# Norm statistics, scan outputs and expert answers moved off VectorE in a four-stage audio tower

## The reference

```
h  = frames(x) @ DCT.T                                  # tokens
u  = layernorm(h)
a  = u + [mamba2(u) , flip(mamba2(flip(u)))] @ proj.T   # two scans, 4 heads, 16 states
h2 = h + layernorm(a)*g + b
y  = sum over the top 2 of 8 experts: w_e * (gelu(layernorm(h2) @ w1_e) @ w2_e)
h3 = h2 + y
h3 = h3 + window_attention(layernorm(h3))               # 8 keys, softmax
h4 = h3 + top-k network(layernorm(h3))                  # keeps 64 of 512, 128 of 256, 64 of 512
```

## Time and profile before

| | us |
|---|---|
| three runs | 8032.64, 7994.39, 8031.15 (median 8031.15) |
| profiled execution, its own time | 8044.3 |
| its span | 8042.4 |
| busy: PE, DVE, ACT, POOL | 6126.0 (76%), 6747.5 (84%), 3593.5 (45%), 2468.3 (31%) |
| mean granted TensorE clock | 0.867 |

### The profile page before, as it was taken

The page is one execution under the profiler, slowest core; times in us unless marked ns, Lnnn a source line. Parts: engine busy times, 40 slices in busy tenths (PEclk is TensorE's granted clock), DMA queues, the critical chain, the costliest instruction groups (busy, mean ns, idle before and its releaser), DMA issues.

```text
span 8042.4 us, 115198 instructions
## 1 busy us (share of the span) xinstructions
PE 6126.0 (76%) x34088; PEld 4811.3 (60%) x34088; DVE 6747.5 (84%) x21836; ACT 3593.5 (45%) x7726; POOL 2468.3 (31%) x2872
## 2 busy tenths in 40 slices
PE   6777787877787777777777778777778777778643
PEld 5656666656666656666656666666666666666422
DVE  2368889888888888889888889888988888888897
ACT  2344445444445444445444445444445444445321
POOL 2233332233332233332233332323332333332220
PEclk8888898888888888898888899888889888889766
DMA  2322222222222222222222222221222222222200
GB/s 71 112 72 67 67 86 78 66 68 67 67 86 78 66 69 65 66 86 79 65 72 65 66 84 79 72 71 59 66 82 79 75 69 63 64 81 80 68 6 4
DMA packets 342571, 560.36 MB, mean 70 GB/s; under 512 B 33728, under 2 KB 261792, under 8 KB 341664
## 3 DMA queue, kind: packets, MB, share of 16 engines
q10 hardware_dynamic: 152576, 357.68, 14.1%
q1 hardware_dynamic: 168992, 153.83, 7.0%
q0 software_dynamic: 20480, 41.98, 1.8%
HBM read 484.63 MB, written 68.74 MB: 69 GB/s over the span
## 4 chain that ended last, share of the span: by engine, by line
PE 36%; DVE 27%; ACT 15%; issue 10%; POOL 6%; ACTq 4%; DMA 2%; POOLq 0%; DVEq 0%; SPq 0%
DVE m L1230 6%; PE pM L656 6%; PE pS L547 5%; PE pM L667 4%; PE pA L709 4%; DVE work L1233 3%; POOL rows L449 3%; DVE sorted L1260 2%; DVE work L1263 2%; ACT hid L915 2%; DVE a L1233 2%; ACTq L895 2%; PE pS L609 2%; PE pS L601 2%; PE pA L721 2%
## 5 line engine op out<-in xcount | busy, mean ns | idle before, releaser
L1230 DVE MAX8 m<-work 128x8 f32<-128x512 f32 x1792 | 1143.6, 680 | 1.0
L547 PE MATMUL pS<-u_fm,wconv_s 128*128 128x315 f32 x3072 | 1015.0, 485 | 94.1 <-ACT xs L860 87.0
L1233 DVE MATCH_REPLACE8 work<-m,work 128x512 f32<-128x512 f32 x1536 | 1026.6, 676 | 0.0
L656 PE MATMUL pM<-turned,expert 128*128 128x128 f32 x4352 | 675.3, 304 | 409.5 <-ACT turned L928 399.2
L410 POOL TENSOR_TENSOR yg<-xs,zs 128x525 f32<-128x525 f32 (+1 forms) x256 | 195.9, 797 | 2489.8 <-ACT xs L870 2489.8
L656 PEld LDWEIGHTS pM<-turned,expert 128*128 128x128 f32 x4352 | 606.2, 213 | 522.5 <-issue 492.5
L547 PEld LDWEIGHTS pS<-u_fm,wconv_s 128*128 128x128 f32 x3072 | 654.0, 217 | 404.6 <-issue 128.3
L915 ACT ACTIVATE hid<-pM,expert 128x128 f32<-128x128 f32 x2176 | 623.2, 372 | 250.5 <-PE pM L656 249.0
L1230 DVE MAX8 m<-a 128x8 f32<-128x512 f32 x768 | 505.4, 679 | 187.9 <-issue 180.9
L667 PE MATMUL pM<-expert,hid 128*128 128x128 f32 x4352 | 629.1, 292 | 0.0
L1263 DVE MATCH_REPLACE8 work<-sorted,work 128x128 f32<-128x128 f32 x2240 | 591.6, 276 | 0.0
(11 more groups left out here) (255 smaller groups left out, 14526.7 us busy)
## 6 DMA issues: line engine op xcount, KB each, us to landing
expert<-in_experts ACTq DMA_DIRECT2D x544, 578.0 KB, 4.0
ab<-decay_rows SPq DMA_DIRECT2D x384, 230.7 KB
rows<-routed_rows SPq DMA_DIRECT2D x128, 256.0 KB, 3.6
answer_rows<-turned ACTq DMA_DIRECT2D x256, 128.0 KB, 3.9
x_sb<-in_x SPq DMA_DIRECT2D x32, 256.0 KB
out<-hk SPq DMA_DIRECT2D x32, 256.0 KB
routed_rows<-un,slot POOLq DMA_INDIRECT x320, 2.2
rows<-answer_rows,slot POOLq DMA_INDIRECT x320, 2.6
```

Of the source, the lines that this page charges most:

```text
L547: last = nc.tensor.matmul(pS[:, 512 * (n % 3):512 * (n % 3) + HQ], wt, tap(d, i, half * HQ, HQ), start=(j == 0), stop=(j == len(blocks) - 1))
L656: last = nc.tensor.matmul(pM[:, bank(i) + j * P:bank(i) + (j + 1) * P], w1_of(i, j), turned[:, (i + 2) % 4, 1, :], start=True, stop=True)
L1230: link(nc.vector.max(m8[:, i, :], now[i]), len(tiles) - 1)
L1233: link(nc.vector.match_replace(work[i], m8[:, i, :], now[i], GONE), len(tiles) - 1)
```

## The change

A helper `act_moments` on ScalarE replaces `moments` on VectorE at four of its five calls (h, h2, h3 twice); the call on `ub` stays. The scan outputs are scaled by ten ScalarE copies into `zs` and added by two GpSimd additions. The gathered answers are weighed by ten ScalarE copies in place and added by two GpSimd additions. All five order strings are new. `x_in` and other semaphores keep their use; `sum1` to `sum3`, `dir_out`, `scaled` and `h3_part` are new.

```diff
+        def act_moments(act, i, first, b, src, spare, var):
+            done = G[f"sum{i + 1}"]
+            for t in range(TILES):
+                last = nc.scalar.activation(spare[:, t, :], src[:, t, :], ACT.Copy, accum_out=lnsum[i][:, 0, t:t + 1])
+            last.then_inc(done.s, 1)
+            act.wait_ge(done.s, done(b, first + 1))
+            nc.scalar.activation(nmean[i][:], lnsum[i][:, 0, :], ACT.Copy, scale=-1.0 / P).then_inc(done.s, 1)
+            act.wait_ge(done.s, done(b, first + 2))
+            for t in range(TILES):
+                last = nc.scalar.activation(spare[:, t, :], src[:, t, :], ACT.Square, bias=nmean[i][:, t:t + 1], accum_out=lnsum[i][:, 1, t:t + 1])
+            last.then_inc(done.s, 1)
+            act.wait_ge(done.s, done(b, first + 3))
+            nc.scalar.activation(vare[i][:, 0:TILES], lnsum[i][:, 1, :], ACT.Identity, bias=c("eps"), scale=1.0 / P).then_inc(var.s, 1)
 def act_stage1
+            act.wait_ge(G["h_sb"].s, G["h_sb"](b, 1))
+            act_moments(act, 0, 0, b, h, u, G["var1"])
...
+            act.wait_ge(G["o_ps"].s, G["o_ps"](b, 1))
+            act.wait_ge(G["rstd1"].s, G["rstd1"](b, 2))
+            for k in range(2 * TILES):
+                d, t = divmod(k, TILES)
+                last = nc.scalar.activation(zs4[:, d, 0, tok(t)], pS[:, tok(k)], ACT.Copy, scale=rstd[0][:, k:k + 1])
+            last.then_inc(G["dir_out"].s, 1)
 def act_stage2
+            act.wait_ge(G["h1_done"].s, G["h1_done"](b, 1))
+            act_moments(act, 1, 0, b, h2, un, G["var2"])
...
+            act.wait_ge(gathered.s, gathered(b, 160))
+            for k in range(2 * TILES):
+                last = nc.scalar.activation(rows[:, k, :], rows[:, k, :], ACT.Copy, scale=top8[:, k % TILES, k // TILES:k // TILES + 1])
+            last.then_inc(G["scaled"].s, 1)
 def act_stage3
+            act.wait_ge(G["u4T_ps"].s, G["u4T_ps"](b, 0))
+            act.wait_ge(G["moe_done"].s, G["moe_done"](b, 1))
+            act_moments(act, 2, 0, b, h3, u3, G["var3"])
...
+            act.wait_ge(G["h3_done"].s, G["h3_done"](b, 2))
+            act_moments(act, 2, 3, b, h3, u3, G["var3"])
 def pool_stage1
+            pool.wait_ge(G["dir_out"].s, G["dir_out"](b, 1))
+            for d in range(2):
+                pool.wait_ge(G["ub"].s, G["ub"](b, d + 1))
+                nc.gpsimd.tensor_tensor(ub[:], ub[:], zs4[:, d, 0, :].rearrange("p (t d) -> p t d", t=TILES), ALU.add).then_inc(G["ub"].s, 1)
 def pool_stage2
+            pool.wait_ge(G["scaled"].s, G["scaled"](b, 1))
+            pool.wait_ge(G["h3_kept"].s, G["h3_kept"](b, 0))
+            pool.wait_ge(G["u4_done"].s, G["u4_done"](b, 0))
+            nc.gpsimd.tensor_tensor(h3[:], h2[:], rows[:, 0:TILES, :], ALU.add).then_inc(G["h3_part"].s, 1)
+            pool.wait_ge(G["h3_part"].s, G["h3_part"](b, 1))
+            nc.gpsimd.tensor_tensor(h3[:], h3[:], rows[:, TILES:, :], ALU.add).then_inc(G["moe_done"].s, 1)
 def dve_stage1
-            dve.wait_ge(G["h_sb"].s, G["h_sb"](b, 1))
-            moments(link, 0, h, G["var1"])
...
-            dve.wait_ge(G["ub"].s, G["ub"](b, 1))
-            dve.wait_ge(G["rstd1"].s, G["rstd1"](b, 2))
-            for d in range(2):
-                for t in range(TILES):
-                    k = d * TILES + t
-                    last = nc.vector.scalar_tensor_tensor(ub[:, t, :], pS[:, tok(k)], rstd[0][:, k:k + 1], ub[:, t, :], ALU.mult, ALU.add)
-                link(last)
+            dve.wait_ge(G["ub"].s, G["ub"](b, 3))
             moments(link, 0, ub, G["var1"])
 def dve_stage2, dve_stage3: three more calls of moments go, and
-            for t in range(TILES):
-                last = nc.vector.scalar_tensor_tensor(h3[:, t, :], rows[:, t, :], top8[:, t, 0:1], h2[:, t, :], ALU.mult, ALU.add)
-            link(last)
-            for t in range(TILES):
-                last = nc.vector.scalar_tensor_tensor(h3[:, t, :], rows[:, TILES + t, :], top8[:, t, 1:2], h3[:, t, :], ALU.mult, ALU.add)
-            last.then_inc(G["moe_done"].s, 1)
```

```diff
-ACT_ORDER = ("44144121211411111411131114113144141111131141131124111322411211121111214112421312142141142112211223111122"
-             "31124244444444244242222422324222432444243224244334444433")
-DVE_ORDER = ("342414424142141142444444444414414444141114111441111111411114111414444444341444414444444344344344342")
-POOL_ORDER = ("21312111313323131")
+ACT_ORDER = ("44443124131333342131311231114111111411411111114111111124111111111111111314413341111424211414122211212131"
+             "23234444144242424234224224224222242222422322244222244444444424")
+DVE_ORDER = ("4444444444141112424342444114141111144414141411411141114311111343444444444144444444444444444414")
+POOL_ORDER = ("3213233111311213211")
...
```

More of the change, by code:

```diff
@@ L61 @@
     ("convb", 6), ("dskip", 4), ("normw", 4), ("projb", P), ("lng", P), ("lnb", P),
-    ("gate_w", E), ("gate_b", E), ("tail", AW * TAIL), ("pos", AW), ("bk", 1),
+    ("gate_w", E), ("gate_b", E), ("tail", AW * TAIL), ("pos", AW), ("bk", 1), ("eps", 1),
     ("wq", P), ("wk", P), ("wv", P),
@@ L77 @@
 COUNTS = dict(
-    x_in=32, xT_ps=1, xT_sb=1, h_ps=1, h_sb=1, var1=3, rstd1=3, u_done=1, uT_ps=1, u_sb=1,
+    sum1=3, sum2=3, sum3=6, x_in=32, xT_ps=1, xT_sb=1, h_ps=1, h_sb=1, var1=3, rstd1=3, u_done=1, uT_ps=1, u_sb=1,
     dt_ps=1, dt_arg=3, dt_act=3, dA_ps=1, dA_sb=1, dA_out=16, ab0=48, ab1=48, ab2=48, ab3=48, proj_ps=HALF_UNITS, proj_sb=HALF_UNITS,
     scanned=12, mix_ps=12, m_done=12, y_ps=12, y_tmp=12, y_gated=2, pad_zero=1, y_sq=2,
-    o_ps=1, ub=1, r_norm=1, attn_scaled=2, h1_done=1,
+    o_ps=1, ub=3, dir_out=1, r_norm=1, attn_scaled=2, h1_done=1,
     var2=1, rstd2=1, u2_done=1, u2T_ps=2, u2T_sb=2, gate_ps=1, gate_arg=1, gate_exp=1,
     chosen=1, rank_ps=1, tiles_done=1, slots_done=1, rows0=48, rows1=32, turned_ps=2, turned_sb=2,
-    expert0=96, expert1=96, expert2=80, hid_ps=MT, hid_sb=MT, tile_done=MT, kept=MT, y_out0=80, y_out1=64, moe_done=1,
+    expert0=96, expert1=96, expert2=80, hid_ps=MT, hid_sb=MT, tile_done=MT, kept=MT, y_out0=80, y_out1=64, scaled=1, h3_part=1, moe_done=1,
     var3=2, rstd3=2, u3_done=1, u3T_ps=2, u3T_sb=2, qkv_ps=6, qkv_sb=6, lg_max=1, lg_done=1, lg_exp=1, den_ps=2, den_sb=2, den_done=1, weighted=2, val_ps=2, att_done=2,
@@ L183, in audio_tower @@
         h = sb("h", [P, TILES, P])
+        lnsum = [sb(f"lnsum{i}", [P, 2, TILES]) for i in range(3)]
         stats = [sb(f"stats{i}", [P, TILES, 6]) for i in range(3)]
@@ L826, in act_stage1 @@
             nc.scalar.copy(h[:].rearrange("p t d -> p (t d)"), pS[:, 0:W]).then_inc(G["h_sb"].s, 1)
+            yield
+            act.wait_ge(G["h_sb"].s, G["h_sb"](b, 1))
+            act_moments(act, 0, 0, b, h, u, G["var1"])
             yield
@@ L1127, in dve_stage2 @@
             link = linker(dve, link2)
-            dve.wait_ge(G["h1_done"].s, G["h1_done"](b, 1))
-            moments(link, 1, h2, G["var2"])
-            yield
             dve.wait_ge(G["gate_ps"].s, G["gate_ps"](b, 1))
@@ L1185, in dve_stage3 @@
             link = linker(dve, link3)
-            dve.wait_ge(G["moe_done"].s, G["moe_done"](b, 1))
-            dve.wait_ge(G["u4_done"].s, G["u4_done"](b, 0))
-            moments(link, 2, h3, G["var3"])
-            yield
             dve.wait_ge(G["qkv_sb"].s, G["qkv_sb"](b, 6))
@@ L1209, in dve_stage3 @@
                 nc.vector.tensor_tensor(att[:, lo:lo + W // 2], pA[:, 0:W // 2], q[:, lo:lo + W // 2], ALU.mult).then_inc(G["att_done"].s, 1)
-            yield
-            dve.wait_ge(G["h3_done"].s, G["h3_done"](b, 2))
-            moments(link, 2, h3, G["var3"])
             dve.sem_clear(link3)
@@ L1346, in constants @@
     return dict(ident=np.eye(P, dtype=np.float32), dct=dct, scan_src=src, live=live, mean256=np.full((P, 1), 1 / 256, np.float32),
-                iota8=np.tile(np.arange(E, dtype=np.float32), (P, 1)),
+                eps=np.full((P, 1), EPS, np.float32), iota8=np.tile(np.arange(E, dtype=np.float32), (P, 1)),
                 iota_tile=np.tile(np.arange(20, dtype=np.float32), (P, 1)), before=np.triu(np.ones((P, P), np.float32), 1),
```

17 lines of the change are left out of this document (8 added, 9 removed).

## The result

| | before | after |
|---|---|---|
| median of the runs | 8031.9 us (4 runs, 7994.39 to 8051.46) | 8496.47 us (4 runs, 8488.44 to 8507.2) |
| ratio, 95% interval | | 1.0585 (1.0545 to 1.0625) |
| span of the profiled execution | 8042.4 | 8493.7 |
| busy: PE, DVE, ACT, POOL | 6126.0, 6747.5, 3593.5, 2468.3 | 6302.2, 6635.6, 3803.9, 2722.6 |

The change made the kernel slower by 5.9%. The forecast of 8112 us (range 7740 to 8290) had the sign and not the size: the time lies outside its range.

A forecast was written before the change was run, and what follows sets the result against it. DVE's own work and a ring through the experts were taken as tight; six legs sum to 241.8 us per turn against 239.0, 29 turns x 2.8 = +81 us on 8044.3, 8125, less 13: 8112 us, range 7740 to 8290.

The forecast's parts named there:

- the ring: Chain through h2, norm, gate, slots, 17 expert tiles, answers, gather, h3, next h2, closing once per turn: 241.8 us against 239.0.
- DVE is left with 196.9 us per turn: DVE's work per turn after 13.0 us of moments, scan sum and expert sum leave its 209.9 us.
- leg B: DVE from stage 1's small steps to the end of the scan: 90 us of work and 5 of waits, 95 us.
- Leg A: Head, from h3 complete to DVE's first small step of stage 1, through ACT's moments and PE's small projection: 29 us.
- zero: The moment when h3 is complete, from which the turn is counted; DVE's first tiles were to start some 4 us ahead.
- Legs C, D, E: Expert tiles from the end of the scan to the last expert copy: 10, 37.5 and 41 us.
- Leg F: Tail, from the last expert copy through gathering, weighing, output DMA, `hk` and two additions to next h3: 29.3 us.
- theory 3: Theory of the follow-up experiments: behind the scan the turn ends with DVE's third level, not with the expert tiles.
- Filling and draining: Six turns without full overlap: filling loses some 10 us as tiles begin late, draining wins 11, nothing net.
- Rival 1: Faster: unseen slack in the head or tiles lets DVE's 13.0 us pass through, 7643 us in full, half 7840; chance 0.33.
- Rival 3: Much slower: PE at its lower clock level in the head and first expert tiles, 8 us per turn, 8350 us; chance 0.12.

The follow-up runs named there:

- POOL quiet: The changed kernel with all 16 GpSimd attention instructions cut to one column: 8215.61 us, 1.0250; the kernel before, cut likewise: 7994.71 us, 0.9967.
- the run with halves: The changed kernel with each of GpSimd's eight attention subtractions of 640 columns cut in two of 320: 8464.98 us, 1.0570 of the kernel before.
- the run with the head alone: The kernel before with only three moments (h3 first, h2, h) moved to ACT, second moments of h3 kept on VectorE: 8279.48 us, 1.0316.
- the one kernel that tried: The changed kernel with second moments of h3, scaled scan outputs and PE's u4 behind the third a3, fifth a3 two tiles earlier: 8690.49 us, 1.0848.
- the old orders with the change: The whole change in the code with the kernel before's order strings, only the moved pieces placed anew: 8598.58 us, 1.0406 of the kernel before.
- the two parts alone: The kernel before with only scan outputs scaled by ACT, added by GpSimd: 8274.27 us, 1.0021; with only answers so weighed and added: 8257.47 us, 1.0015.

## Why the prediction was wrong

- **The step that failed** is the one ahead of the ring: "DVE is left with 196.9 us per turn", and with it leg B's "That leaves 90". It is a sum of durations from the kernel before, taken as if an instruction's time didn't depend on what POOL does beside it. The forecast had named the very move (the attention's subtraction "now stands ahead of the scattering on POOL. It costs the ring nothing") and priced only POOL's time. Measured: DVE busy 99.96 in leg B, 90.41 with POOL quiet. 9.6 us per turn, and the leg 104.2 instead of 95.4 in the means. The runs without the subtraction and without all of POOL's attention work agree on cause and size (DVE busy 186 and 310 us less); the run with halves confirms the cause, the hold by a running instruction, and gained no time.
- A rule would have named the risk, though not its price. *SBUF — State Buffer* of the Trainium skill (Who interferes with whom) says that a VectorE instruction with two SBUF inputs contends with a GpSimd instruction that reads SBUF, that a copy, cast or tensor_scalar in a two-port mode contends with GpSimd too, that the first to issue holds the shared port pair for its whole instruction, and that tensor_reduce never contends. The trace agrees in which instructions are slow and which are not (1.47, 1.61, 1.06, 1.11 us, against 0.31 for the reduction and 0.15 for the one from PSUM). It differs in one thing: a scan waited 11.32 us for eight subtractions, not for one.
- **Leg A** was right in its number (28.6 for 29), and by luck. The prices were right: the accumulating passes took 0.30 and 0.39 us, a moment about 4.25. But the forecast had DVE wait for PE's small projection at 29, with the first three tiles of stage 4 "over by then". It is the other way round: PE and DVE in the order of time, the second line for DVE being the start of stage 1's steps.

```profile
3603.69 2.70 PE L542 MATMUL pS<-cst,u_fm 128*121 128x4 f32 x24 [0.80 <-ACT u_fm L862]
```
```profile
3606.09 2.08 DVE L1261 SCALAR_TENSOR_TENSOR a<-a,m 128x512 f32<-128x512 f32 x3
3608.29 0.21 DVE L1116 TENSOR_TENSOR dtw<-pS,cst 121x48 f32<-121x48 f32 x1
```

  Over 20 turns the projection is over at 26.5 us and DVE's three tiles at 28.5, since they started 1.8 us ahead of zero and not 4. So DVE's own rounds end this head, 2 us behind the chain through the moments, and two errors cancelled. The chain is the bound in the run with the head alone, where three moments cost 3.2%; what they cost in the changed kernel no run shows.
- **Legs C, D, E** were right: 88.1 us for 88.5.
- **Leg F** was mis-sized: 32.0 for 29.3. It was summed over the gathering; the weighing waits instead for the fifth turned tile (`selT`, the selection turned for stage 4's last product). ACT at the end of the turn read, answering to the earlier trace rows:

```profile
3800.46 0.27 ACT L970 COPY turned<-pM 128x128 f32<-128x128 f32 x1 [1.35 <-PE pM L681]
...
3816.77 0.59 ACT L1069 COPY selT<-pD 128x512 f32<-128x512 f32 x1 [7.16 <-PE pD L810]
...
3821.42 0.59 ACT L1069 COPY selT<-pD 128x512 f32<-128x512 f32 x1 [1.21 <-PE pD L810]
3821.90 3.03 ACT L985 ACTIVATE rows<-rows,top 128x128 f32<-128x128 f32 x10
3824.83 0.25 ACT L1072 COPY hk<-pD 128x128 f32<-128x128 f32 x1
```

  The fourth turned tile (3816.77) waits for DVE's last selection, which starts at 3814.74; the gathering was over at 3816.4, the weighing starts at 3821.9. The ten weighing copies took 3.03 us, not 2.7. DVE's wait for the third level's values was forecast (14 us, 14.12 in this turn), but I didn't follow it to the tail. So theory 3 holds for the tail: what ends it is DVE's third level. With POOL quiet leg F is as long (32.1), so the contention has no part in it.
- **Filling and draining** were not "nothing net": h3 is first complete at 322 us instead of 304, and from the last one to the end it takes 386 instead of 374, together 29 us. With POOL quiet the two are 325 and 375 us, against 302 and 369 in the kernel before with POOL quiet: the loss in filling stays, and the one in draining falls from 11.5 to 6 us.
- Check of the sum: 31 turns at 251.2 instead of 237.5 us (all of them, the early ones too) are 422, and 29 make 451; the spans differ by 451.
- **The rivals.** Rival 1 (13 us of DVE pass through) did not come: leg B got 7 us shorter, in spite of the contention, and 15.9 with POOL quiet, about as the forecast itself had it, and legs A, C to E and F gave it all back. How much of B's gain is the moved work and how much the expert tiles that now come behind the scan isn't separated. Rival 3, the clock, did not decide: 0.88 in leg B against 0.91 before, and 0.93 with POOL quiet, in a stretch where DVE is the bound.
- One reading of the prediction needs a word: the 2.8 us of idle time of the earlier trace rows stand ahead of the 154 table loads. Behind the loads the trace shows none either: the next pass starts 0.01 us after a load in the median of all 789.
- Left open: what of leg F could be had back, since the one kernel that tried moved the work to a worse place; and whether the 4% of the old orders with the change is the same on every chip, since it was measured on one where the kernel before takes 2.8% longer.

## What to carry to other kernels

Before moving work to GpSimd, or only its place in GpSimd's order, list what VectorE runs in that stretch: here two-input operations from SBUF (comparisons, products, maxima), scans, casts and scalings were held up, searches and reductions were not, and most of the price fell on VectorE's side (310 us of busy time, and 56 on GpSimd's). Work taken from the busiest engine was worth nothing while the ring closed later (ratios of 1.002 for the two parts alone), and what was added at the head of that ring counted in full (6.7 us of head in the run with the head alone, a turn at least 7.6 us longer). A leg that comes out right can do so for the wrong reason: look which engine ends it. The gain that was there lay in a wait (one Gelu behind three DMA issues), not in the busy shares.

## What was not expected of the hardware

- A VectorE scan of 1.17 us, started while GpSimd ran eight back-to-back 128x640 subtractions, took 11.32 us and ended with the streak. The small instructions got through after one subtraction each.
- A VectorE comparison on one partition and 160 elements (0.31 us) takes 1.56 us in the mean beside them, and one of 128x384 beside the multiplications 1.80 instead of 0.55: the same 1.25 us is lost by both, so by share small instructions lose most.
- ScalarE's scaled copies of 128x128 took 3.03 us for ten in a row; an accumulating pass shows 0.30 us with its accumulator read (0.19) overlapping the next pass, every 0.29 us.
- The kernel before took 8255 us in the median on one chip and 8012 to 8032 in the other series.
